# Attention and expert layer on one core: the order of ScalarE's high parts, GpSimd's low parts and scattered rows, and SyncE's copy of k

## The chip, the core and the metric

The kernel runs on one core of one Trainium2 chip. The metric is the device time of one execution in microseconds (us); of several executions the median is given. All times below are of that kind or come from one profiled execution.

## The reference, cut to what matters

The input x is 4 sequences of 512 tokens with 256 features. Attention has 32 query heads and 8 key/value heads of 64 features; both q and k are rotated by position. It is followed by a mixture of 8 experts with two chosen per token.

```
proj = layernorm(x) @ W_qkv
q, k, v = split(proj);  q = rope(q);  k = rope(k)
attn = einsum('bqhmd,bkhd->bhmqk', q, k) / 8
attn = where(q_pos >= k_pos and q_pos < k_pos + 64, -inf, attn)
w = softmax(concat([attn, sink]))[..., :-1]
x = x + einsum('bhmqk,bkhd->bqhmd', w, v).reshape(B, L, 2048) @ W_out
# experts: softmax gates, top 2 of 8, capacity 640 rows per expert
h = relu(rows_of_expert @ w1 + b1);  y = h @ w2 + b2
x = x + sum over the two experts of weight * y
```

Every large product is made of float32 operands split in a high part (rounded to the matmul's fp32r type) and a low part (the rest): three matmuls, high by high, low by high and high by low, stand for one.

## The kernel before

**Groups.** Attention is cut into 32 groups g (4 sequences by 8 key/value heads). A group has one key head, one value head and four query heads. Its projection comes in three chunks of 128 rows by 512 tokens: KV (k in rows 0 to 63, v in rows 64 to 127), Q01 and Q23 (two query heads each). Scores are made in 16 units of 128x512, two by two on TensorE (L1591), each followed by one VectorE instruction that masks and takes the maximum (L1185) and by one exponential on ScalarE (L895). VectorE then transposes pairs of units (L1196), and TensorE multiplies by v (L1617) and by W_out (L1649).

**The order written by hand.** Function `all_periods` (L364) walks g and a unit number n from 0 to 15. At each it calls, for each engine, the step of group g at n, then that of group g + 1 at n - 16, of g - 1 at n + 16 and of g - 2 at n + 32, then the routing of a finished sequence and other early work. So an entry "-15: KV" of a table stands in unit 1 of the group before. Each engine runs its own instructions in this order, and waits on semaphores in between; an entry sets an order on one engine and no time. I call the 16 units of group g "the period of g".

**The path of a chunk.** TensorE projects KV and Q01 of g + 1 in units 0 and 2 (`project_pair`, L1508) and Q23 in unit 10 (`project`, L1495, which waits for v's copy `s_v_next`). ScalarE copies each chunk out of PSUM into chunk_sb (`chunk_out`, L862, instruction L871). SyncE moves 16-row halves of it to swap_sb (`swap_halves`, L505, DMAs L511: two for KV, four for Q01 and Q23). GpSimd rotates: two products and one sum, L709, L710 and L714. ScalarE makes the high part (`qk_high`, L882, instruction L886), GpSimd the low part (`qk_low`, L717, instruction L720). k is needed in both halves of the partitions, so SyncE copies rows 0 to 63 of k's parts, 256 KB, to rows 64 to 127 (`k_twice`, L514, DMA L517). The first score of a group (L1591, n == 0) waits for Q01's low part, for that copy and for the maximum of the unit before. TensorE's product with v of the group before starts in unit 4 and waits, on its way, for the KV chunk's copy (L1611), since both use one PSUM bank.

**v.** ScalarE copies the turned v (`v_copy`, L879) in unit 9; SyncE writes it to memory and reads it back spread over partitions (L538, L546).

**SyncE's queue** per period, in order: reciprocals out and spread (L554, L562) of the group before, swaps of KV and Q01, in the first sequence weight loads and the writing of the weight parts, v out and in, swaps of Q23, then for the groups 8 to 31 the reading of the weight's high and low parts (`load_w_again`, L525, DMAs L530, two of 384 KB, issued three groups ahead), then `k_twice`:

```
                swap_halves(g + 1, Q23)
                if NKV <= g + 3 < GROUPS:
                    load_w_again(g + 3, (g + 3) % 2)
                k_twice(g + 1, (g + 1) % 2)
```

24 of the 31 copies of k stand behind such a pair of reads.

**ScalarE's queue** in a period, as far as the change goes: exponential 1, KV chunk out (g + 1), exponential 2, exponential 3, high part of Q23 (g), Q01 chunk out, ..., exponential 7, high part of k, exponentials 8 and 9, v's copy, exponential 10, high part of Q01, exponential 11, Q23 chunk out.

**GpSimd's queue**: denominator (L745), rotation and low part of Q23 (g), rotations of KV and Q01 (g + 1), low parts of k (unit 6) and of Q01 (unit 10), residual of g - 2 (L752, two instructions, unit 11), a weight's low part in the first sequence, sink argument (L735). `SCATTER_AT`, `ROOT_AT` and `GATE_EXP_AT` place the routing of a finished sequence, which runs beside the next one's eight groups: r counts its units, so r = 67 is unit 3 of the fifth group. `ROOT_AT` is a run of seven small GpSimd instructions (L765 to L772), `GATE_EXP_AT` eight small ScalarE instructions in two lots (L1072, L1074), `SCATTER_AT` eight indirect DMAs that GpSimd issues (L800), each with a wait for the spread reciprocals of an earlier group. `LATE_ROOT_AT` places two more such runs on GpSimd.

After the last group the routing of the last sequence and the eight experts run; the change moves no instruction there.

Of the kernel before, what the change touches and what calls it, by code (L numbers as in the profile page):

```python
# [39 lines left out]
UNITS = QM * TPB  # L40
# [15 lines left out]
KV, Q01, Q23 = 0, 1, 2  # L56
# [4 lines left out]
def moe_layer(nc, x, w_qkv, w_out, sink, gate_w, w1, b1, w2, b2, rope, out):  # L61
    ctx = ExitStack()
    with ctx:
# [276 lines left out]

        PROJ_PAIR_AT = {-16: 0, -14: 1}
        PROJ_AT = {-6: Q23}
        CHUNK_OUT_AT = {-15: KV, -13: Q01, -5: Q23}
        TURN_V_AT, V_NEXT_AT = -8, -7
        ROT_AT = {2: Q23, -12: KV, -11: Q01}
        QK_HI_AT, QK_LO_AT = {3: Q23, -9: KV, -6: Q01}, {3: Q23, -10: KV, -6: Q01}
        W_HI_AT, SPLIT_AT, SECOND_SPLIT_AT = -7, -3, -10
        PV_AT, at = {}, 0
        for n, blocks in [(20, 5), (22, 5), (24, 6)]:
# [3 lines left out]
        SINK_AT, DENOM_AT, RECIP_AT = 15, 16, 17  # L353
        HEADS_AT = 25
        Y_AT = {28: 0, 30: 1}
        Y_FIRST_OUT_AT, Y_OUT_AT, RESIDUAL_AT = 30, 31, 43
        ODD_ORDER = (1, 0)
        LAST_RESIDUAL_AT = {29: 0, 31: 1}

# [27 lines left out]
        LOGITS_AT, MEAN_PART_AT, STD_AT, TURN_LOGITS_AT, CENTRE_AT = 52, 53, 53, 54, 55  # L387
        TOP_AT, INDEX_AT = 56, 57
        ONEHOT_AT, COUNT_AT, RSTD_AT, PLACE_AT = 69, 70, 70, 71
        INV_STD_AT, ROOT_AT = 58, 67  # L390
        NORM2_AT, GATE_EXP_AT = {87: 0, 88: 1, 90: 2, 91: 3}, {71: (0, 1), 73: (2, 3)}
        SELECT_AT = 72
        PICK_AT, INDICES_AT, WEIGHTS_AT = 85, 86, 86
        SCATTER_AT = {89: (0, 1), 99: (2,), 105: (3, 4), 115: (5,), 121: (6, 7)}
        ROUTE_STEPS = 122

        def mean_part_of(eng):
# [19 lines left out]
        LATE_VAR_AT = {UNITS + 5: 0, 6 * UNITS + 5: 1}  # L417
        LATE_STD_AT = {UNITS + 5: 0, 6 * UNITS + 7: 1}
        LATE_INV_AT = {UNITS + 10: 0, 6 * UNITS + 10: 1}
        LATE_ROOT_AT = {2 * UNITS + 3: 0, 7 * UNITS + 3: 1}  # L420
        LATE_PERIODS = [3, 4, 5, 6, 8, 9, 13, 14, 15, 16, 17, 22]
        LATE_NORM_AT = {p * UNITS + 2: i for i, p in enumerate(LATE_PERIODS)}
        LATE_TURN_AT = {p * UNITS + 4: i for i, p in enumerate(LATE_PERIODS)}
# [50 lines left out]
        def rotated(q):  # L474

            return q - CHUNKS + 1
# [9 lines left out]
        def _(sp):  # L486
# [6 lines left out]
            def load_w(g, j):  # L493

                if later(g - 1):
                    sp.wait_ge(s_w_lo, g - 1)
                k = g % NKV
                sp.dma_start(w_raw[j][:, :, 0:QM * HD],
                             w_rows[:, :, bass.ds(k * (QM * HD), QM * HD)]).then_inc(s_w_in[j], 16)
                sp.dma_start(w_raw[j][:, :, QM * HD:QM * HD + HD],  # L500
                             w_rows[:, :, bass.ds(k * HD + QW, HD)]).then_inc(s_w_in[j], 16)
                sp.dma_start(w_raw[j][:, :, QM * HD + HD:GW],
                             w_rows[:, :, bass.ds(k * HD + (QW + KW), HD)]).then_inc(s_w_in[j], 16)

            def swap_halves(g, c):  # L505

                q = g * CHUNKS + c
                sp.wait_ge(s_chunk_out, q + 1)
                for base in (0,) if c == KV else (0, HD):
                    for to, of in ((0, HD // 2), (HD // 2, 0)):  # L510
                        sp.dma_start(swap_sb[c][base + to:base + to + RH, :],  # L511
                                     chunk_sb[c][base + of:base + of + RH, :]).then_inc(s_swapped[c], 16)

            def k_twice(g, j):  # L514

                sp.wait_ge(s_qk_lo, rotated(g * CHUNKS + KV))
                sp.dma_start(qk[j][HD:P, :, PAIRS, :].bitcast(F32), qk[j][0:HD, :, PAIRS, :].bitcast(F32)).then_inc(s_k_twice, 16)  # L517

            def keep_w(g, j):

                sp.wait_ge(s_w_lo, g + 1)
                for part, w in enumerate((w_hi, w_lo)):
                    sp.dma_start(w_parts[g, part], w[j][:, :, :].rearrange("p c n -> p (c n)").bitcast(F32)).then_inc(s_w_kept[j], 16)
# [9 lines left out]
            def v_out(g):  # L533

                sp.wait_ge(s_v_next, g + 1)
                if g > 0:
                    sp.wait_ge(s_v_in[(g - 1) % 2], ((g - 1) // 2 + 1) * (16 * QUADS))
                sp.dma_start(v_rows, v_next[:, :, :].rearrange("p t d -> p (t d)")).then_inc(s_v_out, 16)  # L538

            def v_in(g, j):  # L540

                sp.wait_ge(s_v_out, g * 16 + 16)
                if later(g - 1):
                    sp.wait_ge(s_pv, g - 1 + 1)
                for a in range(QUADS):
                    sp.dma_start(v_quads[j][a * BLK:(a + 1) * BLK, :, :],  # L546
                                 v_rows.rearrange("(c j) n -> j c n", j=BLK)).then_inc(s_v_in[j], 16)

            def recip_out(g):

                sp.wait_ge(s_recip, g + 1)
                if g > 0:
                    sp.wait_ge(s_recip_in, g * 32)
                sp.dma_start(recip_rows, recip_t[:, :]).then_inc(s_recip_out, 16)  # L554

            def recip_spread(g):

                sp.wait_ge(s_recip_out, g * 16 + 16)
                if later(2 * g):
                    sp.wait_ge(s_heads, 2 * g + 1)  # L560
                for p in range(PAIRS):
                    sp.dma_start(recip_wide[p * HD:(p + 1) * HD, :, :].rearrange("p a (c i) -> p a c i", i=BLK),  # L562
                                 recip_rows.rearrange("(x a c) i -> x a c i", x=1, a=QUADS)[:, :, p * 8:p * 8 + 8, :]
                                 .broadcast_to([HD, QUADS, 8, BLK])).then_inc(s_recip_in, 16)
# [14 lines left out]
            def out_init(b):  # L579

                sp.wait_ge(s_residual, (b + 1) * 2 * NKV)
                sp.dma_start(out_rows[:, b * TPB:(b + 1) * TPB, :],
                             x_sb[:, b * TPB:(b + 1) * TPB, :]).then_inc(s_out_init, 16)

            for g in range(GROUPS - 1):
                if g > 0:
                    recip_out(g - 1)
                    recip_spread(g - 1)
                swap_halves(g + 1, KV)
                swap_halves(g + 1, Q01)  # L590
                if g + 1 < NKV:
                    keep_w(g + 1, (g + 1) % 2)
                if g + 3 < NKV:
                    load_w(g + 3, (g + 3) % 2)
                v_out(g + 1)
                v_in(g + 1, (g + 1) % 2)
                swap_halves(g + 1, Q23)
                if NKV <= g + 3 < GROUPS:
                    load_w_again(g + 3, (g + 3) % 2)
                k_twice(g + 1, (g + 1) % 2)  # L600
                if g % NKV == 1 and g > NKV:
                    out_init(g // NKV - 1)

# [41 lines left out]
        def _(pool):  # L645
# [128 lines left out]
            def pool_route(r, b, last):  # L774
# [10 lines left out]
                if r == IDS_AT:  # L785
                    if b > 0:
                        pool.wait_ge(s_scattered, b * (16 * TPB * TOPK))
                    nc.gpsimd.iota(xn2[:, :, D:D + 1].bitcast(U32), pattern=[[P, TPB], [0, 1]], base=b * L,
                                   channel_multiplier=1).then_inc(s_ids, 1)
                for c in SCATTER_AT.get(r, ()):  # L790
                    if not last:
# [22 lines left out]
            def pool_ahead(m):  # L814
                if m in LATE_ROOT_AT:
                    i = LATE_ROOT_AT[m]
                    part = LATE_PARTS[i]
# [27 lines left out]
        def _(act):  # L845
# [42 lines left out]
            def act_step(n, g, j):  # L888
                if n in CHUNK_OUT_AT:
                    chunk_out(g, CHUNK_OUT_AT[n])  # L890
                if n == V_NEXT_AT:
# [954 lines left out]
```

## Time and profile before

| what | value |
|---|---|
| median of 3 runs | 1327.89 us (1326.34 to 1331.36) |
| profiled execution: its own time | 1333.01 us |
| profiled execution: span from first to last instruction | 1331.2 us |
| mean granted TensorE clock | 0.905 of full |
| TensorE (PE) busy | 1077.3 us, 81% of the span |
| VectorE (DVE) busy | 934.6 us, 70% |
| GpSimd (POOL) busy | 711.1 us, 53% |
| ScalarE (ACT) busy | 708.6 us, 53% |
| chain that ended last, by engine | PE 45%, issue 13%, DMA 13%, POOL 8%, ACT 8%, DVE 7%, SyncE's queue 5% |

PE, DVE, ACT and POOL are the four computing engines, SP is SyncE, and a q behind a name means the engine's sequencer, which issues DMAs. A timeline row gives the start in us from the span's start, the length in us, engine, line, operation, what is written from what is read, the shapes and the count; in square brackets stand the idle time of the engine before it and what ended that time. The profiled execution is 0.4% longer than the median of the runs.

### The profile page before, as it was taken

Reading aid. Unit: us, or ns where it says so; the run is one execution under the profiler, and the core shown is the slowest. Engines: PE = TensorE matmul, PEld = TensorE weight load, DVE = VectorE, ACT = ScalarE, POOL = GpSimd, SP = SyncE. Lnnn points to the kernel's source line nnn. Section 1 sums busy time; section 2 is a strip of 40 time slices with the busy share of each in tenths; the row PEclk is TensorE's granted clock in tenths of the full one; section 3 lists DMA queues with packets and bytes.
Section 4 is the critical chain, followed back from the end, with each engine's and each line's share of the span. In section 5 each row is a group of like instructions: output and inputs, shape, how many; then the busy total and the mean of one; then the engine's idle time right before and its main releaser. Section 6 shows DMA issues by size and latency. Waiting matters only on the chain.

```text
span 1331.2 us, 33592 instructions
## 1 busy us (share of the span) xinstructions
PE 1077.3 (81%) x13509; PEld 844.5 (63%) x13509; DVE 934.6 (70%) x1962; ACT 708.6 (53%) x1769; POOL 711.1 (53%) x646
## 2 busy tenths in 40 slices
PE   7778777777687688787877777787777989999997
PEld 4457555555465566665665555565555669999996
DVE  7788777666577777776777676767677567777664
ACT  5566655555365455654665555546555445554442
POOL 4677664555455556654565666545557523224332
PEclk9899888888788888988888888888889999999998
DMA  5544543433322233323222333323333244433441
GB/s 146 148 119 138 147 125 106 109 100 92 88 74 82 72 92 95 103 81 92 77 81 73 100 99 97 106 83 88 83 99 84 69 165 110 111 100 100 106 105 21
DMA packets 107195, 131.98 MB, mean 99 GB/s; under 512 B 22848, under 2 KB 85376, under 8 KB 106912
## 3 DMA queue, kind: packets, MB, share of 16 engines
q1 hardware_dynamic: 89264, 110.08, 28.9%
q0 software_dynamic: 7296, 8.55, 3.9%
q10 hardware_dynamic: 10480, 11.20, 2.8%
q8 instruction: 107, 1.75, 0.5%
q14 instruction: 48, 0.39, 0.1%
HBM read 84.28 MB, written 28.12 MB: 84 GB/s over the span
## 4 chain that ended last, share of the span: by engine, by line
PE 45%; issue 13%; DMA 13%; POOL 8%; ACT 8%; DVE 7%; SPq 5%; ACTq 0%; POOLq 0%; DVEq 0%
PE bank L1782 9%; PE bank L1591 8%; DMA swap_sb<-chunk_sb 6%; PE bank L1649 6%; PE bank L1793 5%; PE bank L1617 5%; PE bank L1524 4%; ACT probs_ring L895 4%; DMA qk<-qk 4%; PE bank L1504 3%; SPq L511 3%; PE bank L1796 3%; POOL chunk_sb L714 2%; POOL chunk_sb L709 2%; POOL swap_sb L710 2%
## 5 line engine op out<-in xcount | busy, mean ns | idle before, releaser
L1185 DVE CUSTOM_DVE_ANT_0 probs_ring<-bank,mask,sink_neg 128x512 f32<-128x512 f32 x512 | 361.8, 740 | 244.4 <-PE bank L1591 233.5
L895 ACT ACTIVATE probs_ring<-probs_ring,neg_max 128x512 f32<-128x512 f32 x512 | 364.8, 714 | 296.6 <-DVE neg_max L1185 293.8
L1591 PE MATMUL bank<-qk 64*128 64x512 f32 x1488 | 266.7, 466 | 178.6 <-issue 112.8
L1196 DVE STREAM_TRANSPOSE probs_t<-probs_ring 128x1024 f32<-128x1024 f32 x256 | 317.4, 1240 | 6.2 <-ACT probs_ring L895 5.9
L1591 PEld LDWEIGHTS bank<-qk 64*128 64x128 f32 x1488 | 151.6, 212 | 253.6 <-issue 215.4
L720 POOL TENSOR_TENSOR qk<-chunk_sb,qk 128x512 fp32r<-128x512 f32 (+1 forms) x93 | 119.1, 1284 | 287.8 <-ACT qk L886 287.5
L1617 PE MATMUL bank<-probs_t,v_quads 32*64 32x256 f32 x8192 | 259.9, 388 | 3.9 <-issue 0.3
L1617 PEld LDWEIGHTS bank<-probs_t,v_quads 32*64 32x64 f32 x8192 | 189.9, 134 | 57.8 <-issue 37.4
L835 POOL DMA_INDIRECT out<-expert_sb,slots x40 | 77.5, 1938 | 154.1 <-DVE expert_sb L1448 147.4
L709 POOL TENSOR_TENSOR chunk_sb<-chunk_sb,rope_sb 128x512 f32<-128x512 f32 (+1 forms) x94 | 119.7, 1273 | 73.7 <-DMA swap_sb<-chunk_sb 73.4
L714 POOL TENSOR_TENSOR chunk_sb<-chunk_sb,swap_sb 128x512 f32<-128x512 f32 (+1 forms) x93 | 118.6, 1276 | 7.3
L710 POOL TENSOR_TENSOR swap_sb<-swap_sb,rope_sb 128x512 f32<-128x512 f32 (+1 forms) x94 | 119.7, 1273 | 0.0
L1104 ACT ACTIVATE hidden<-bank,b_sb 128x320 f32<-128x320 f32 x128 | 60.5, 525 | 110.5 <-PE bank L1782 107.7
L1649 PE MATMUL bank<-wo_sb,heads_sb 64*128 64x256 f32 x992 | 118.1, 378 | 0.0
L1793 PE MATMUL bank<-w_part,hidden_hi 128*128 128x512 f32 x320 | 114.9, 400 | 0.0
L1524 PE MATMUL bank<-xcur,w_hi 64*128 64x512 f32 x496 | 106.9, 507 | 0.0
L1649 PEld LDWEIGHTS bank<-wo_sb,heads_sb 64*128 64x128 f32 x992 | 96.4, 189 | 14.5
L886 ACT ACTIVATE qk<-chunk_sb 128x512 fp32r<-128x512 f32 (+1 forms) x93 | 57.9, 622 | 79.5 <-POOL chunk_sb L714 79.3
L895 ACT ACTIVATION_READ_ACCUMULATOR probs_ring<-probs_ring,neg_max 128x1 f32 x512 | 96.1, 188 | 0.0
L871 ACT ACTIVATE chunk_sb<-bank 128x512 f32<-128x512 f32 x94 | 55.0, 585 | 76.8 <-PE bank L1524 75.4
L1796 PE MATMUL bank<-w_part,hidden_lo 128*128 128x256 f32 x320 | 90.1, 282 | 0.0
L752 POOL TENSOR_TENSOR x_sb<-x_sb,y_sb 128x512 f32<-128x512 f32 x62 | 79.4, 1280 | 4.4
(193 smaller groups left out, 1545.4 us busy)
## 6 DMA issues: line engine op xcount, KB each, us to landing
v_quads<-v_rows SPq DMA_DIRECT2D x128, 128.0 KB
recip_wide<-recip_rows SPq DMA_DIRECT2D x64, 256.0 KB, 4.4
w_raw<-in_L_ffn_w SPq DMA_DIRECT2D x14, 1024.0 KB, 8.7
swap_sb<-chunk_sb SPq DMA_DIRECT2D x314, 32.0 KB, 2.5
w_hi<-w_parts SPq DMA_DIRECT2D x24, 384.0 KB, 3.5
w_lo<-w_parts SPq DMA_DIRECT2D x24, 384.0 KB, 4.8
qk<-qk SPq DMA_DIRECT2D x31, 256.0 KB, 4.9
slots<-slot_rows SPq DMA_DIRECT2D x9, 662.5 KB, 4.0
```

The costliest lines, as they stand in the source:

```text
L709: nc.gpsimd.tensor_tensor(straight, straight, rope_sb[rows, 0, :], ALU.mult).then_inc(s_pool, 1)
L710: nc.gpsimd.tensor_tensor(swapped, swapped, rope_sb[rows, 1, :], ALU.mult).then_inc(s_pool, 1)
L714: nc.gpsimd.tensor_tensor(qk_first[:, c - Q01, :] if g == 0 else straight, straight, swapped, ALU.add).then_inc(s_rot, 1)
L895: nc.scalar.activation(probs[(g * UNITS + n) % RING][:, :], probs[(g * UNITS + n) % RING][:, :], ACT.Exp, bias=neg_max[j][:, n:n + 1], sca ...
L1185: nc.vector.tensor_tensor_reduce(probs[(g * UNITS + n) % RING][:, :], SCORE[SCORE_OF[n // 2][n % 2]][:, :], mask[:, L - P - t * P:2 * L - ...
L1196: nc.vector.transpose(probs_t[:, pair_slot(g, h // 2), :, :] .rearrange("p b (h q) -> p h b q", h=2)[:, :, :, t * BLK:(t + 1) * BLK], prob ...
L1524: ins = nc.tensor.matmul(chunk_bank(c)[:, :], w[rows, kc, chunk_cols(c)], xcur[g // NKV % 2][rows, part, kc, :], start=(second == 0 and kc ...
L1591: ins = nc.tensor.matmul(out_bank, qk[j][half, q_part, h // 2, t * P:(t + 1) * P], qk[j][half, k_part, PAIRS, :], start=(m == 0), stop=(m ...
L1617: ins = nc.tensor.matmul(PV[a][p * HD:(p + 1) * HD, 0:2 * P], v_quads[j][rows, d, c * HD:(c + 1) * HD], probs_t[rows, pair_slot(g, p), blk ...
L1649: ins = nc.tensor.matmul(PV[a][:, 0:D], heads_sb[rows, a, h * P:(h + 1) * P], wo_sb[rows, (g % NKV) * 2 + h, :], start=(half == 0 and h == ...
L1793: nc.tensor.matmul(FFN2[s][:, :], hidden_hi[:, c, s * P:(s + 1) * P], w2_parts[e % 2][:, c, :, :].rearrange("p t d -> p (t d)"), start=(c ...
L1796: ins = nc.tensor.matmul(FFN2[s][:, 0:D], hidden_lo[:, c, s * P:(s + 1) * P], w2_hi[e % 2][:, c, :], start=False, stop=(c == HC - 1))
```

## The change

It moves entries of the hand-written order. ScalarE: KV chunk out from unit 1 to unit 2, the high part of Q23 from unit 3 to 2 (there it comes ahead of the KV chunk), the high part of k from 7 to 8 (behind exponential 8). GpSimd: the low part of Q01 from unit 10 to 7, the residual from 11 to 8, the routing's root from unit 3 to 6 of its period, the scatters of r = 99 and 115 to 91 and 107 (from unit 3 of a period to unit 11 of the one before), the two late roots by four units. ScalarE's gate exponentials go from units 7 and 9 to 12 and 14. SyncE issues k's copy ahead of the two reads of weight parts.

```
-        CHUNK_OUT_AT = {-15: KV, -13: Q01, -5: Q23}
+        CHUNK_OUT_AT = {-14: KV, -13: Q01, -5: Q23}
-        QK_HI_AT, QK_LO_AT = {3: Q23, -9: KV, -6: Q01}, {3: Q23, -10: KV, -6: Q01}
+        QK_HI_AT, QK_LO_AT = {2: Q23, -8: KV, -6: Q01}, {3: Q23, -10: KV, -9: Q01}
-        Y_FIRST_OUT_AT, Y_OUT_AT, RESIDUAL_AT = 30, 31, 43
+        Y_FIRST_OUT_AT, Y_OUT_AT, RESIDUAL_AT = 30, 31, 40
-        INV_STD_AT, ROOT_AT = 58, 67
-        NORM2_AT, GATE_EXP_AT = {87: 0, 88: 1, 90: 2, 91: 3}, {71: (0, 1), 73: (2, 3)}
+        INV_STD_AT, ROOT_AT = 58, 70
+        NORM2_AT, GATE_EXP_AT = {87: 0, 88: 1, 90: 2, 91: 3}, {76: (0, 1), 78: (2, 3)}
-        SCATTER_AT = {89: (0, 1), 99: (2,), 105: (3, 4), 115: (5,), 121: (6, 7)}
+        SCATTER_AT = {89: (0, 1), 91: (2,), 105: (3, 4), 107: (5,), 121: (6, 7)}
-        LATE_ROOT_AT = {2 * UNITS + 3: 0, 7 * UNITS + 3: 1}
+        LATE_ROOT_AT = {2 * UNITS + 7: 0, 7 * UNITS + 7: 1}
...
                 swap_halves(g + 1, Q23)
+                k_twice(g + 1, (g + 1) % 2)
                 if NKV <= g + 3 < GROUPS:
                     load_w_again(g + 3, (g + 3) % 2)
-                k_twice(g + 1, (g + 1) % 2)
```

## Rows read from the trace of the kernel before

**Rows 1.** Waits: who waited for what, us in total, times, longest us.

```profile
PE bank L1591 <- issue: 112.8, 21, 8.5
...
POOL chunk_sb L709 <- DMA swap_sb<-chunk_sb: 73.4, 33, 7.6
PE bank L1591 <- DMA qk<-qk: 56.0, 10, 9.0
```

**Rows 2.** Timeline of PE, 541 to 577 us, the period of group 16.

```profile
542.20 1.65 PE L1591 MATMUL bank<-qk 64*128 64x512 f32 x6 [5.28 <-issue]
...
548.83 2.42 PE L1617 MATMUL bank<-probs_t,v_quads 32*64 32x256 f32 x80
...
561.04 0.73 PE L1504 MATMUL bank<-xcur,w_hi 128*128 128x512 f32 x2 [0.91 <-ACT v_next L879]
...
573.38 1.65 PE L1591 MATMUL bank<-qk 64*128 64x512 f32 x6 [5.65 <-issue]
```

**Rows 3.** Timeline of SyncE's queue in the same stretch.

```profile
549.60 4.67 SPq L511 DMA_DIRECT2D swap_sb<-chunk_sb  x6
...
564.49 2.42 SPq L511 DMA_DIRECT2D swap_sb<-chunk_sb  x4
567.01 0.53 SPq L530 DMA_DIRECT2D w_hi<-w_parts  x1
...
568.06 0.67 SPq L517 DMA_DIRECT2D qk<-qk  x1
```

**Rows 4.** k's copy in the stretches 370:970, 190:340 (5 copies), 568.1:568.2, 990:1030 (2), 40:170 (5).

```profile
L517 SPq DMA_DIRECT2D qk<-qk x19: 660/661/665, 372.4 to 963.4; - x19
...
DMA to landing us min/median/max: 4.4/4.9/5.6
...
DMA to landing us min/median/max: 5.8/6.8/7.0
...
DMA to landing us min/median/max: 5.2/5.2/5.2
...
DMA to landing us min/median/max: 3.1/3.1/3.1
...
DMA to landing us min/median/max: 3.1/4.1/5.4
```

**Rows 5.** Timeline of ACT, 541 to 577 us.

```profile
548.09 0.60 ACT L871 ACTIVATE chunk_sb<-bank 128x512 f32<-128x512 f32 x1 [1.92 <-PE bank L1524]
...
550.49 0.61 ACT L886 ACTIVATE qk<-chunk_sb 128x512 fp32r<-128x512 f32 x1
...
558.67 0.63 ACT L886 ACTIVATE qk<-chunk_sb 64x512 fp32r<-64x512 f32 x1 [2.74 <-POOL chunk_sb L714]
...
560.62 0.36 ACT L879 ACTIVATE v_next<-bank 128x256 f32<-128x256 f32 x1
```

**Rows 6.** Timeline of DVE, unit 2 of group 16.

```profile
546.75 0.71 DVE L1185 CUSTOM_DVE_ANT_0 probs_ring<-bank,mask,sink_neg 128x512 f32<-128x512 f32 x1
```

**Rows 7.** Timeline of POOL: k's rotation, Q01's last step, a scatter, group 30's Q23.

```profile
554.78 1.28 POOL L709 TENSOR_TENSOR chunk_sb<-chunk_sb,rope_sb 64x512 f32<-64x512 f32 x1 [2.32 <-DMA swap_sb<-chunk_sb]
...
561.19 1.30 POOL L714 TENSOR_TENSOR chunk_sb<-chunk_sb,swap_sb 128x512 f32<-128x512 f32 x1
...
522.94 1.01 POOL L800 DMA_INDIRECT slot_rows<-xn,scatter_idx  x1 [1.62 <-DMA swap_sb<-chunk_sb]
...
1001.00 1.29 POOL L714 TENSOR_TENSOR chunk_sb<-chunk_sb,swap_sb 128x512 f32<-128x512 f32 x1
```

**Rows 8.** Timeline of ACT around the first gate exponentials, group 12.

```profile
426.21 0.38 ACT L1072 ACTIVATE gates<-logits,neg_top,rstd 128x8 f32<-128x8 f32 x1
...
427.71 0.70 ACT L895 ACTIVATE probs_ring<-probs_ring,neg_max 128x512 f32<-128x512 f32 x1
```

**Rows 9.** Busy time by stretch: PE, PEld, DVE, ACT, POOL, then granted clock, DMA.

```profile
573.40:579.40 6.00, 6.00 (x28) 5.14 (x30) 3.46 (x8) 1.52 (x4) 0.00 (x0) 0.50 0.02 3
997.90:1003.90 6.00, 5.80 (x59) 4.88 (x67) 5.05 (x13) 4.03 (x13) 4.04 (x4) 1.00 0.03 7
```

## The prediction

> **What bounds the kernel now.** I read the waits first: of everything TensorE waits for in the attention part, the first score of a group stands out, with 112.8 us in 21 waits put down to "issue" and 56.0 us in 10 put down to k's copy [rows 1]. Together that is 168.8 us in 31 waits, one for each of the 31 copies. Are they one thing? The timeline of one period says so. TensorE starts group 17 at 573.38 us after 5.65 us of nothing, that is, its last work ended at 567.73 [rows 2]. SyncE issued the copy at 568.06 [rows 3], and it landed 5.2 us later, at 573.26 [rows 4]: 0.12 us before the score. So "issue" hides the same wait, and each group starts when k's second half has landed.
>
> What holds the copy? In SyncE's queue it comes last: four swaps of Q23 from 564.49, the two reads of weight parts from 567.01, then the copy [rows 3]. k itself is long ready: its rotation began at 554.78 and GpSimd's rotation of Q01 was done at 562.49 [rows 7], with k's low part next in its queue. The reads cost the copy twice: their issue, 568.06 - 567.01 = 1.05 us, and the transfer, for the copy's 256 KB go behind 768 KB. The 19 copies behind such reads from group 10 on land in 4.4/4.9/5.6 us, the two last ones, which have none ahead, in 3.1 [rows 4].
>
> **The change, part by part.** The sum is made against the profiled execution, 1333.0 us.
>
> *k's copy ahead of the weight parts.* 24 copies gain 1.05 us of issue: 25.2 us. Their landing shortens too. For the 19 the ends are 3.1 us (as the two without reads) and 4.9 (as now, if packets issued 0.7 us later still share the way). I take 3.4, close to the lower end, since what is issued ahead of the copy is then just what stands ahead of the two at 3.1: 19 x 1.5 = 28.5 us. The five copies from 190 to 340 us land in 6.8 us in the median [rows 4]; there ScalarE also writes zero rows. The five copies before them, with no read ahead but partly beside such writes, take 3.1/4.1/5.4. The ends are 3.1 and 6.8, and I take 4.7: 5 x 2.1 = 10.5 us. Sum 64.2 us. The reads now land about when the next group starts, two periods ahead of their use, and the swaps on which the next chain rests go out 7.4 us after such a start (549.60 - 542.20, [rows 2, 3]): nobody waits. What is late next: TensorE's own work ends at 567.73; the copy, issued at 567.01 and landed at 570.4, still comes 2.7 us later. So the copy stays the bound and the gain is kept whole.
>
> The Trainium skill ("DMA: Bandwidth & Descriptors", Queues, rings and completion order) says that each engine takes descriptors in ring order, but that data descriptors carry no barrier. By the ring order alone the 19 would land in 3.1 us and give 5.7 us more; by free mixing they would stay at 4.9. The trace agrees with the order as far as 3.1 against 4.9 goes; no run here yet shows reads issued behind a copy.
>
> *ScalarE: KV out behind exponential 2 and Q23's high part.* VectorE ends unit 2 at 547.46 [rows 6]. An exponential of 0.70 [rows 8] and the high part's 0.61 [rows 5] follow, so KV's copy starts near 548.8 instead of 548.09 [rows 5]: 0.7 us late. Two wait for it. TensorE's product with v started at 548.83, 0.14 us behind the copy's end [rows 2, 5], and moves by 0.7. SyncE's first swap went out at 549.60 [rows 3], the copy now ends near 549.4, so it does not move here; where TensorE's clock is low and unit 2 ends later it would, by up to 0.5.
>
> *k's high part behind exponential 8.* ScalarE waited 2.74 us for the rotation [rows 5]; exponential 8 now fits into that, and v's copy comes 0.70 us earlier, at 559.9. TensorE waited 0.91 us for it [rows 2], so that takes up the 0.7 us that it lost. And Q23's chunk is copied behind Q01's high part, which waits for GpSimd until 562.49 [rows 7], and nothing here moved that. So in this period both edits cancel. In others the v path or TensorE decides. Bounds per period: -0.3 (0.7 less for v against 0.4 more on the swap's path) and +0.7, for 30 periods -9 and +21; I take +0.15 each, the value nearest to this period's: +5 us.
>
> *GpSimd.* In an ordinary period the new numbers change no order: nothing stands between units 7 and 11 but the low part and the residual. So "low parts behind both rotations" is true already: cost 0, covered by nothing, as there is nothing to cover. Only the routing's pieces really move. Two scatters per routed sequence, six in all, stood ahead of k's rotation, 1.01 us each [rows 7], partly while GpSimd waited for the swap anyway: up to 6 us, I take 2. The new place is behind the residual, where GpSimd has slack until the sink argument. The gate exponentials, first lot 427.71 - 426.21 = 1.5 us [rows 8], stood ahead of exponential 8 and v's copy in three periods: up to 4.5 us, I take 3. The roots stood just ahead of a rotation, where GpSimd waits for a swap anyway, 73.4 us in 33 waits or 2.2 us each [rows 1]; moved behind the rotations, their seven small instructions bring between 0 and, had that wait been used up, their own length; I take 0. The residual ahead of scatters that wait: 0.
>
> Sum: 64.2 - 5 + 2 + 3 = 64 us, so 1269 us for that execution. The median of the runs was 0.4% (5.1 us) lower, so I give 1327.9 - 64 = **1264 us**.
>
> **The rivals.** *The landing does not shorten* (8%): reads issued 0.7 us behind the copy share its way. Then only the issue is won, 25 us: 1303 us. For it: all use the same 16 engines. Against: the bytes ahead of the copy are gone, and 3.1 us is what it takes without them.
>
> *The clock rises too* (9%). A group now starts at the lower level, 1.2 GHz, after some 5.7 us of idle: 0.50 in the first 6 us; at the start of group 30, whose copy had landed in 3.1 us, it stayed at 1.00, 2.4 GHz [rows 4, 9]. With 2.7 us of idle some starts may stay high. The first six matmuls took 1.65 us at the low level [rows 2], half of that could go: with the units behind them about 0.8 us in 24 periods, 19 us, 1245 us. Against: the low stretch may only move into the middle of the period. The Trainium skill ("TensorE: Matmul & The Clock Gate", HAM oscillation) tells of this kind of loss from waits between bursts; by it the shorter wait would help, which rows 9 neither show nor exclude for 2.7 us.
>
> *The copy is not what releases the score* (4%): something else always comes 0.1 us before. Then the time is 1328 + 5, no change. Against: 31 waits for 31 copies, and the 0.12 us between landing and score.
>
> *Slower* (2%): Q23's high part now stands ahead of KV out, and its rotation ends late when groups start early. In group 30 it ended at 1002.29 [rows 7], 4.4 us after TensorE's start at 997.9 [rows 9]. ScalarE now wants it 6.0 us after the start (547.46 + 0.70 against 542.20, [rows 2, 6, 8]), somewhat sooner at the high clock. Beyond that each us is paid by KV out, its swap and the whole next chain. The sign turns where that wait passes 64 / 30 = 2.1 us, at a rotation end of 8.1 us: at 9.2 us the price is 3.2 x 30 = 96 us against 64, 1360 us. Against: nothing in the change delays Q23's swaps.
>
> **The numbers.** My forecast holds 77%, with its own range from the bounds: the 19 landings at 3.1 (6 us) and ScalarE's edits at -0.2 per period (10 us), to all landings 0.6 us longer (14 us) and ScalarE's edits at +0.5 (11 us): 1248 to 1289. All terms at their ends at once would give 1231 (landings 14, ScalarE 14, GpSimd and gates 5 us) and 1324 (39, 16 and 5), which is wider than 8 in 10 asks for. The range 1244 to 1289 takes the clock case in and leaves out the unshortened landing, no change, and slower: 14%, plus tails. About 0.5% is what a measurement of this kernel can tell from no change. Faster by more: 77 + 8 + 9 = 94%; same 4%, slower 2%.
>
> **What would show it.** In the changed profile: k's copies issued right behind the swaps of Q23, all landing near 3.4 us; TensorE's waits ahead of the first score down from 169 to about 105 us; periods of ordinary groups of 28 to 29 us instead of 31.2 (573.38 - 542.20, [rows 2]); KV out 0.7 us later in its period, with the product with v as well, and v's copy 0.7 earlier; no scatter ahead of a rotation. I am wrong if the copies still take 4.9 us, if the score is released by anything else, or if ScalarE waits for Q23's rotation in unit 2.

## The result, and the profile after

The changed kernel takes **1217.46 us** (median of 3 runs, 1217.24 to 1218.3) against 1327.89: ratio 0.9173 [0.9139, 0.9208]. The forecast was 1264, with a range from 1244 to 1289. The direction was right, the size was not: the gain is 110 us, not 64, and the time lies 27 us below the range.

The head of the changed kernel's page (cut):

```profile
span 1215.5 us, 33592 instructions
...
PE 1045.4 (86%) x13509; PEld 832.0 (68%) x13509; DVE 928.1 (76%) x1962; ACT 710.0 (58%) x1769; POOL 713.5 (59%) x646
```

TensorE's busy time fell by 32 us (1077.3 before) though it does the same work: it ran at a higher clock, 0.941 of full speed granted against 0.905.

Waits of the changed kernel, to hold against [rows 1]:

```profile
PE bank L1591 <- DMA qk<-qk: 78.4, 23, 4.8
PE bank L1591 <- issue: 28.0, 8, 4.6
PE bank L1617 <- ACT chunk_sb L871: 20.9, 30, 1.6
PE bank L1504 <- ACT v_next L879: 12.9, 9, 6.5
```

The first scores wait 106.4 us in 31 waits, where 168.8 stood: the forecast said "about 105". Of the fourth row it gave no sum. Here are that row and one more of the kernel before; the second matters below:

```profile
PE bank L1504 <- ACT v_next L879: 34.1, 21, 5.8
...
PE bank L1542 <- ACT x2T L1064: 8.2, 3, 3.0
```

k's copy in the changed kernel, in 190:330 (5 copies) and 330:870 (19), to hold against [rows 4]:

```profile
L517 SPq DMA_DIRECT2D qk<-qk x5: 654/655/1176, 193.2 to 310.6; - x5
DMA to landing us min/median/max: 3.2/3.4/4.9
...
L517 SPq DMA_DIRECT2D qk<-qk x19: 654/655/659, 341.9 to 855.9; - x19
DMA to landing us min/median/max: 3.1/3.2/3.3
```

The same period of group 16, SyncE's queue and then TensorE, to hold against [rows 2, 3]:

```profile
512.62 2.42 SPq L511 DMA_DIRECT2D swap_sb<-chunk_sb  x4
515.08 0.65 SPq L517 DMA_DIRECT2D qk<-qk  x1
515.83 0.54 SPq L530 DMA_DIRECT2D w_hi<-w_parts  x1
```

```profile
490.53 0.97 PE L1591 MATMUL bank<-qk 64*128 64x512 f32 x6 [3.09 <-DMA qk<-qk]
...
493.57 1.54 PE L1591 MATMUL bank<-qk 64*128 64x512 f32 x6
...
497.85 2.42 PE L1617 MATMUL bank<-probs_t,v_quads 32*64 32x256 f32 x80 [0.62 <-ACT chunk_sb L871]
...
518.39 1.21 PE L1591 MATMUL bank<-qk 64*128 64x512 f32 x6 [3.06 <-DMA qk<-qk]
```

The period is 518.39 - 490.53 = 27.86 us long, 31.18 before and 28 to 29 in the forecast; the copy stands right behind the swaps. From group start to the copy's issue it takes 24.55 us (25.86 before), from there to the next start 3.31 (5.32 before). The first six matmuls take 0.97 us, not 1.65: this group starts at 2.4 GHz. The half speed comes later: the scores at 493.57 took 1.54 us, and the first six microseconds stand at a granted clock of 0.72, not at 0.50 as in [rows 9]:

```profile
490.40:496.40 6.00, 5.87 (x38) 5.52 (x40) 4.25 (x10) 2.90 (x9) 4.00 (x4) 0.72 0.43 160
```

Not every group is like this one. I call a start cold when its first six matmuls took over 1.3 us (1.65 is the value at 1.2 GHz, 0.97 that at 2.4). Of the 31 starts 28 were cold before and 17 still are. Idle of 3.03 us ahead of group 15 was followed by 1.65 us, idle of 3.09 us ahead of group 16 by 0.97.

The chain from start to start can be summed over the 30 full periods of a trace, in three pieces: from a group's first VectorE instruction to the issue of k's copy, from there to the copy's landing (the last arrival recorded for its semaphore), and from there to the next group's first VectorE instruction. In us, with the cold starts beside:

| kernel | start to issue | issue to landing | landing to start | sum | cold starts of 31 |
|---|---|---|---|---|---|
| before | 774.8 | 149.7 | 50.2 | 974.7 | 28 |
| changed | 723.8 | 100.2 | 42.3 | 866.2 | 17 |
| e1, copy alone | 749.2 | 104.4 | 38.8 | 892.4 | 12 |
| e2, k's high part alone | 756.1 | 149.3 | 50.3 | 955.8 | 28 |
| e3, all but the copy | 760.2 | 154.0 | 50.5 | 964.6 | 28 |
| e4, all but k's high part | 748.9 | 103.3 | 40.7 | 892.8 | 15 |
| e10, one read ahead | 746.2 | 134.4 | 50.8 | 931.3 | 29 |
| e11, filling matmuls | 711.4 | 101.1 | 33.1 | 845.6 | 2 |

Between the kernel before and the changed one, start to issue fell by 51 us, issue to landing by 49.5, landing to start by 8. The sum of 108.5, with some 7 us ahead of and behind these periods, is the difference of the spans, 1331.2 - 1215.5 = 115.7. In both traces all 31 first scores start 0.1 us after the landing of k's copy.

### The profile page after: what moved, and what is told of

Its sections match the earlier page's. It is cut to its first block and busy times, and to the rows that moved or that the text cites. A ratio compares the mean times of both kernels' runs of the same rounds, so it can differ in the third digit from the quotient of the medians.

```text
span 1215.5 us, 33592 instructions
## 1 busy us (share of the span) xinstructions
PE 1045.4 (86%) x13509; PEld 832.0 (68%) x13509; DVE 928.1 (76%) x1962; ACT 710.0 (58%) x1769; POOL 713.5 (59%) x646
## 5 line engine op out<-in xcount | busy, mean ns | idle before, releaser
L1591 PE MATMUL bank<-qk 64*128 64x512 f32 x1488 | 259.4, 454 | 112.0 <-DMA qk<-qk 78.4
L1591 PEld LDWEIGHTS bank<-qk 64*128 64x128 f32 x1488 | 148.0, 204 | 183.4 <-issue 147.7
L1617 PE MATMUL bank<-probs_t,v_quads 32*64 32x256 f32 x8192 | 249.1, 380 | 23.9 <-ACT chunk_sb L871 20.9
L1617 PEld LDWEIGHTS bank<-probs_t,v_quads 32*64 32x64 f32 x8192 | 186.6, 132 | 71.0 <-DVE probs_t L1196 32.9
L720 POOL TENSOR_TENSOR qk<-chunk_sb,qk 128x512 fp32r<-128x512 f32 (+1 forms) x93 | 118.7, 1281 | 108.5 <-ACT qk L886 108.3
L714 POOL TENSOR_TENSOR chunk_sb<-chunk_sb,swap_sb 128x512 f32<-128x512 f32 (+1 forms) x93 | 119.3, 1283 | 7.3
L710 POOL TENSOR_TENSOR swap_sb<-swap_sb,rope_sb 128x512 f32<-128x512 f32 (+1 forms) x94 | 120.5, 1282 | 0.0
L1524 PE MATMUL bank<-xcur,w_hi 64*128 64x512 f32 x496 | 103.4, 486 | 0.0
L1782 PE MATMUL bank<-slots_hi,w_hi 128*128 128x320 f32 x256 | 79.4, 310 | 0.0
L1782 PE MATMUL bank<-slots_lo,w_hi 128*128 128x320 f32 x256 | 79.0, 308 | 0.0
```

What stands on the lines that cost most here:

```text
L710: nc.gpsimd.tensor_tensor(swapped, swapped, rope_sb[rows, 1, :], ALU.mult).then_inc(s_pool, 1)
L714: nc.gpsimd.tensor_tensor(qk_first[:, c - Q01, :] if g == 0 else straight, straight, swapped, ALU.add).then_inc(s_rot, 1)
L1591: ins = nc.tensor.matmul(out_bank, qk[j][half, q_part, h // 2, t * P:(t + 1) * P], qk[j][half, k_part, PAIRS, :], start=(m == 0), stop=(m ...
L1617: ins = nc.tensor.matmul(PV[a][p * HD:(p + 1) * HD, 0:2 * P], v_quads[j][rows, d, c * HD:(c + 1) * HD], probs_t[rows, pair_slot(g, p), blk ...
L1782: ins = nc.tensor.matmul(banks[4 + 2 * (c % 2) + half][:, 0:HALF], w[:, kc, c * P:(c + 1) * P], a[:, at:at + HALF], start=(kc == 0 and m = ...
```

## The experiments

They ran in four batches, each beside runs of the kernel before on the same chip (medians 1331.77, 1340.82, 1333.75 and 1336.55 us), so ratios are compared, not times. Two add matmuls whose result is not used, e11 and e15; all others only reorder.

### Which edit carries the gain

**e1**, the kernel before with the copy's edit alone:

```diff
                 swap_halves(g + 1, Q23)
+                k_twice(g + 1, (g + 1) % 2)
                 if NKV <= g + 3 < GROUPS:
                     load_w_again(g + 3, (g + 3) % 2)
-                k_twice(g + 1, (g + 1) % 2)
```

> The kernel before with k's copy ahead of the two reads of weight parts, and nothing else. Theory A (each edit has its own part): the order of the copy gives the landings (about 48 us over 24 copies), the issue (25 us) and a little of TensorE's clock at the group starts (up to 8 us), so 73 to 81 us of the 110: 1247 to 1255 us. Rival B (the earlier start alone shifts everything, ScalarE's and GpSimd's edits do nothing): 1215 to 1225 us. Rival C (the forecast on record for this part, landings of 3.4 and 4.7 us): 64 us, 1264 us.

**e3**, the changed kernel with SyncE's order put back:

> The changed kernel with the copy of k put back behind the reads. Theory A: the gain of all but the copy, 110 - 77 = about 33 us, shows alone: 1288 to 1302 us. Rival B: nothing of it without the copy's edit: 1322 to 1332 us. Forecast on record for these parts: 1328 us.

**e2**, the kernel before with k's high part behind exponential 8, and **e4**, the changed kernel with it back in unit 7:

```diff
-        QK_HI_AT, QK_LO_AT = {3: Q23, -9: KV, -6: Q01}, {3: Q23, -10: KV, -6: Q01}
+        QK_HI_AT, QK_LO_AT = {3: Q23, -8: KV, -6: Q01}, {3: Q23, -10: KV, -6: Q01}
```

> The kernel before with only the high part of k moved from unit 7 to unit 8 on ScalarE. Theory A: what stood behind its wait in unit 7 (the turned x of three periods, norms, gate exponentials) is released, about 4 us in each of three periods with x turned, 1 to 2 us in the three with gate exponentials, and some of an exponential's 0.7 us elsewhere: 15 to 25 us faster, 1303 to 1313 us. Rival (forecast on record: the edits on ScalarE cancel): 1323 to 1333 us.

> The changed kernel with k's high part back in unit 7. Theory A: it loses 15 to 25 us, 1232 to 1243 us, with TensorE waiting about 3 us for the second turned x in the periods of groups 10, 18 and 26 again. Rival B: same time as the changed kernel, 1215 to 1221 us.

| kernel | ratio to before | interval |
|---|---|---|
| changed | 0.9173 | 0.9139 to 0.9208 |
| e1, copy alone | 0.9352 | 0.9285 to 0.9419 |
| e3, all but the copy | 0.9848 | 0.9777 to 0.9919 |
| e2, k's high part alone | 0.984 | 0.9777 to 0.9904 |
| e4, all but k's high part | 0.9338 | 0.9273 to 0.9404 |

The copy's edit is worth 1 - 0.9352 = 0.0648, 86 us of 1331.77, by itself, and 0.9848 - 0.9173 = 0.0675, 90 us, on top of the others. k's high part is worth 0.016 and 0.0165, 21 and 22 us, where the forecast had let it cancel with KV out and booked a loss of 5 for both. 86 + 21 = 107 of 110 us: the two edits carry nearly the whole gain, and they add. The intervals of these four runs reach 0.006 to 0.007 to either side, some 9 us, so the 21 us can be told from no effect, but their size is rough. e2 and e4 came out as expected. On the scale of the first runs, e1 (1242 us) was 5 us faster than its theory, and e3 (1308) missed its 1288 to 1302. With the copy's edit alone the waits are these:

```profile
PE bank L1504 <- ACT v_next L879: 52.3, 23, 7.7
PE bank L1591 <- issue: 47.5, 22, 4.8
PE bank L1591 <- DMA qk<-qk: 32.1, 8, 5.4
```

First scores 79.6 us in 30 waits. But Q23's projection (L1504) now waits 52.3 us for v's copy, 34.1 before: what k's copy gave up, v's copy partly took. In e2 that wait is 17.0 us in 14, but the first scores there wait 186.8 us in 32, 18 more than before: in e2 an earlier projection of Q23 mostly met a copy of k that was not earlier.

**e5 and e16**, the changed kernel with KV out and Q23's high part put back; **e6 and e17**, with all of GpSimd's entries and the gates put back. Each was run twice in different batches, and **e14** is the changed kernel once more:

```diff
-        CHUNK_OUT_AT = {-14: KV, -13: Q01, -5: Q23}
-        QK_HI_AT, QK_LO_AT = {2: Q23, -8: KV, -6: Q01}, {3: Q23, -10: KV, -9: Q01}
+        CHUNK_OUT_AT = {-15: KV, -13: Q01, -5: Q23}
+        QK_HI_AT, QK_LO_AT = {3: Q23, -8: KV, -6: Q01}, {3: Q23, -10: KV, -9: Q01}
```

> The changed kernel with KV's chunk out back in unit 1 and Q23's high part back in unit 3. Forecast on record: these edits cost about 0.15 us per period (bounds -0.3 to +0.7 together with k's high part), so undoing them gives up to 15 us, 1203 to 1215 us. Rival (nothing waits for them): 1215 to 1220 us, with TensorE's product with v again 0.14 us behind KV's copy and starting 0.6 us sooner in its period. Second rival (they help, as exponential 2 no longer waits): 1222 us or more.

> The changed kernel with KV out in unit 1 and Q23's high part in unit 3, against the changed kernel on the same chip. TensorE's product with v waits 21 us in all for KV's copy in the changed kernel, but most of that is taken up by later waits: 0 to 8 us faster (ratio 0.911 to 0.917). If this edit had been a gain: ratio above 0.920.

> The changed kernel with all of GpSimd's entries and the gate exponentials as before (low part of Q01, residual, roots, gate exponentials, scatters); ScalarE's KV out and high parts and the order of k's copy stay changed. Forecast on record: 5 us (scatters 2, gates 3), so 1222 us. Theory A: k's high part in unit 8 has already released what the gate exponentials held up (they now come after the wait is used up), 1217 to 1221 us. Rival (GpSimd's order matters): 1230 us or more.

> The changed kernel with GpSimd's entries and the gate exponentials as before, against the changed kernel on the same chip: 3 to 13 us slower (ratio 0.919 to 0.927). If they do nothing: 0.915 to 0.919.

> The changed kernel itself, beside the three others on one chip, as their reference: a ratio of 0.917 to the kernel before within its interval.

Measured: e5 0.9127 [0.9078, 0.9176], e16 0.9149 [0.9103, 0.9195]; e6 0.9197 [0.9144, 0.9249], e17 0.9209 [0.9169, 0.9249]; e14 0.9178 [0.9142, 0.9214]. Against 0.9173 and 0.9178, ScalarE's edit looks like a loss of 0.003 to 0.005 (4 to 6 us) and GpSimd's like a gain of 0.002 to 0.003 (3 to 4 us). Every interval overlaps the changed kernel's, so neither is told apart from nothing. The traces say a little more. The sum over the 30 periods is 866.2 and 866.4 us in the two profiles of the changed kernel, 861.4 and 866.6 in those of e5 and e16, and 878.9 in both of e6 and e17: GpSimd's edits with the gates lean to a gain, of some 4 us by the ratios and 13 by these four profiles. Which of its five edits would bring it, no run separates.

### Why k's high part is worth 21 us

The forecast looked at an ordinary period. Periods in which a sequence is routed have one more piece behind k's high part in ScalarE's queue: the second half of the turned x (L1064, unit 7). TensorE's turn of v (L1542) stands behind it. Group 10 of the kernel before, ScalarE and then TensorE:

```profile
356.81 0.63 ACT L886 ACTIVATE qk<-chunk_sb 64x512 fp32r<-64x512 f32 x1 [2.49 <-POOL chunk_sb L714]
357.35 0.57 ACT L1064 ACTIVATE x2T<-bank 128x512 f32<-128x512 f32 x1
```

```profile
358.07 0.66 PE L1542 MATMUL bank<-identity,chunk_sb 64*128 64x64 f32 x4 [2.98 <-ACT x2T L1064]
358.65 5.42 PE L1617 MATMUL bank<-probs_t,v_quads 32*64 32x256 f32 x96
```

ScalarE waited 2.49 us for GpSimd's rotation of k with the turned x standing behind it in the queue, TensorE waited 2.98 us for that piece, and then its 96 matmuls took 5.42 us, at 1.2 GHz. In the changed kernel the piece goes first, and the same 96 take 2.85. The window of the kernel before (granted clock 0.50), then ScalarE and TensorE of the changed kernel:

```profile
357.50:364.10 6.60, 6.03 (x102) 3.64 (x102) 0.32 (x1) 2.10 (x6) 4.33 (x5) 0.50 0.06 22
```

```profile
330.76 0.57 ACT L1064 ACTIVATE x2T<-bank 128x512 f32<-128x512 f32 x1
...
333.24 0.62 ACT L886 ACTIVATE qk<-chunk_sb 64x512 fp32r<-64x512 f32 x1
```

```profile
331.48 0.43 PE L1542 MATMUL bank<-identity,chunk_sb 64*128 64x64 f32 x4
331.85 2.85 PE L1617 MATMUL bank<-probs_t,v_quads 32*64 32x256 f32 x96
```

**e8** tests that reading from the other side. k's high part stays, and the turned x is put ahead of it in the kernel before:

```diff
-        TURN_X_AT, X2T_AT = {36: 0, 38: 1}, {37: 0, 39: 1}
+        TURN_X_AT, X2T_AT = {36: 0, 38: 1}, {37: 0, 38: 1}
```

> The kernel before with only the second half of the turned x (ScalarE's copy L1064) moved from unit 7 to unit 6 of its period, ahead of k's high part. If that copy behind k's wait is what stops TensorE in the periods of groups 10, 18 and 26 (2.98 us idle in the first, and a product with v at the low clock behind it), they lose about 4 us each as in the run with k's high part in unit 8 (4.6, 3.6, 3.6): 12 us, about 1315 to 1320 us, and those periods are 31 to 33.5 us long. If k's high part has to move itself, nothing: 1327 to 1333 us.

Measured 0.9902 [0.9869, 0.9936], 13 us (9 to 18). Group 10 of e8:

```profile
357.03 0.60 ACT L1064 ACTIVATE x2T<-bank 128x512 f32<-128x512 f32 x1 [1.75 <-PE bank L1708]
...
358.78 0.63 ACT L886 ACTIVATE qk<-chunk_sb 64x512 fp32r<-64x512 f32 x1 [0.45 <-POOL chunk_sb L714]
```

The three periods themselves show it, from one group's first score to the next one's, in us:

| group | before | e2 | e8 |
|---|---|---|---|
| 10 | 37.15 | 32.55 | 33.22 |
| 18 | 35.93 | 32.38 | 32.17 |
| 26 | 34.75 | 31.12 | 30.75 |
| sum gained | | 11.8 | 11.7 |

So the piece queued behind k's high part is worth 12 us in either run. The 30 periods of e2 gain 18.9 us together. Of the other 7.1, 4.5 fall in group 13 (36.79 before, 32.28 in e2) and 2.6 in the other 26 periods together, 0.1 each. Some 7 us of the difference between those two profiles lie outside the periods. In the changed order it is otherwise: e4 loses 26.6 us against the changed kernel, 13.0 in groups 10, 18 and 26 and the rest spread over others, with 21.6 us of waits for v's copy where 12.9 stood. That v's copy carries that rest is likely, but no run separates it.

Group 13 stays in part unexplained. A small VectorE instruction there took 3.49 us before and 0.19 in the changed kernel:

```profile
457.65 3.49 DVE L406 TENSOR_TENSOR xn<-gates,top_sum 128x32 f32<-128x32 f32 x1
```

```profile
416.01 0.19 DVE L406 TENSOR_TENSOR xn<-gates,top_sum 128x32 f32<-128x32 f32 x1
```

Before, GpSimd's rotation of k ran beside it. In the traces of all runs but e15 this instruction took 0.88 us or more (1.03 in e2, 1.12 in e8) wherever the second or third step of a rotation (L710, L714) ran beside it, and 0.19 everywhere else. That is only observed; no run separates it, and the changed kernel taken once more (e14) has 1.12 in group 13. Its 3.49 - 1.03 = 2.5 us are over half of what e2 gained in that period.

### How much the reads cost, and the clock

**e10**, the changed kernel with the first read (384 KB) ahead of the copy and the second behind it:

> The changed kernel with the read of the high weight parts (384 KB) again ahead of k's copy, that of the low parts behind it: half the dose. If issue and bytes ahead set the landing, the copy goes out 0.57 us later and lands in about 4.2 us instead of 3.2, so each of 24 periods is 1.5 us longer, 36 us, plus a few us of clock at the starts: 1250 to 1260 us. If only the place in the queue's issue counts and not the bytes: 14 us, 1231 us. If the step from two reads to one brings nothing (a threshold): 1300 us.

Measured 0.9614 [0.9574, 0.9654], 0.0441 more than the changed kernel, 59 us for one read in 24 periods. SyncE's queue and TensorE in e10:

```profile
609.94 0.53 SPq L531 DMA_DIRECT2D w_hi<-w_parts  x1
610.51 0.66 SPq L517 DMA_DIRECT2D qk<-qk  x1
611.26 0.54 SPq L531 DMA_DIRECT2D w_lo<-w_parts  x1
```

```profile
614.97 1.65 PE L1594 MATMUL bank<-qk 64*128 64x512 f32 x6 [4.80 <-DMA qk<-qk]
```

(The edit adds three lines to the kernel, so L1591 is L1594 here.) In this period the start comes 4.46 us after the issue, not 3.3, and after 4.80 us of idle it runs at 1.2 GHz: 1.65 us. Over all 30 periods, by the table of pieces, e10 is longer than the changed kernel by 22 us from start to issue (24 x 0.57 = 14 of them are the read's own issue), by 34 from issue to landing, and by 8 from landing to start: 65 us in the profiled executions, 59 by the ratios. e10's copies land in 4.6 us in the median, those of the changed kernel in 3.2. The expectation, 36 us and a little of clock, was missed: it had 1.0 us more per landing and little for the clock. The landings took 1.4 us more, and 29 of 31 starts are cold, where 17 were.

The second read adds 33 us in the same sums (e3 against e10): 14, 20 and nothing. So the first read costs two thirds of what both do: more than half of issue and landing, and the whole of the clock at the starts.

**e11** fills the wait ahead of each first score with matmuls whose result is not used:

```diff
+                            pe.wait_ge(s_chunk_out, (g + 1) * CHUNKS)
+                            keep_warm(2, PROJ, rope_sb[:, 0, :])
```

> The changed kernel with two more matmuls (identity by a constant table, into the projection's free bank, result unused) ahead of each group's first score, in TensorE's wait for k's copy. Theory on the clock: the idle stretch of some 3 us is what lets the granted clock fall to 1.2 GHz at the starts; filled, the starts run at 2.4 GHz and the first six matmuls take 1.0 instead of 1.65 us in the 18 or so periods where they were slow: 10 to 20 us faster, 1198 to 1207 us. Rival (the dummies hold up the score, or the low stretch moves elsewhere): 1215 to 1225 us.

Measured 0.9008 [0.8959, 0.9058], 0.0165 or 22 us faster than the changed kernel. The wait for the copy is still there, issue to landing as long as before (101.1 us against 100.2) and each first score 0.1 us behind a landing. What the filling gave back is the half speed behind the waits: 2 cold starts, not 17. The granted clock is 0.979:

```profile
core 0: 1198.9 us, clock 0.979
```

### A better place for the copy

In the changed kernel the copy still stands behind Q23's four swaps, 2.42 us of issue. **e12** puts it ahead of them. **e13** does so too and puts KV out and Q23's high part back to units 1 and 3. **e15** is e13 with one filling matmul ahead of each first score, where e11 has two.

```diff
+                k_twice(g + 1, (g + 1) % 2)
                 swap_halves(g + 1, Q23)
-                k_twice(g + 1, (g + 1) % 2)
```

> The changed kernel with k's copy one place further ahead, before the four swaps of Q23. k's low part is ready about 20 us into a period and the swaps begin at 21, so the copy would go out 2.4 us sooner and land at about 24.4 us, near the end of TensorE's own work at 24.5 to 25. If the copy is still the bound, 1.5 to 2.5 us per period in 30 periods: 45 to 75 us, 1142 to 1172 us. Rival (Q23's rotation, now 0.7 us later and with earlier starts, holds ScalarE in unit 2, where KV out waits behind it): half of it is given back, 1180 to 1200 us.

> The same with KV's chunk out back in unit 1 and Q23's high part back in unit 3, so nothing stands behind Q23's rotation in unit 2. If that rotation holds ScalarE in the run before this one, this one is 10 to 30 us faster than it; if it does not, they are equal within 5 us.

> k's copy ahead of Q23's swaps, KV out in unit 1 and Q23's high part in unit 3, with one more matmul ahead of each group's first score. In the run without it the gaps ahead of the first score are down to about 1 us and the clock is at 2.4 GHz nearly always, so the clock theory expects nothing more from it: ratio within 0.005 of that run's 0.857. Rival (any filling still helps): 0.845 or less. If the dummy now holds up the score, 0.865 or more.

Measured: e12 0.8994 [0.895, 0.9038], 1200.86 us; e13 **0.8574 [0.8541, 0.8608], 1141.59 us**; e15 0.8535 [0.8503, 0.8568], 1139.7 us. e13 beats both kernels clearly; e15's interval overlaps e13's, so filling adds nothing there that can be told apart. For e12 the expectation was 1142 to 1172 us; its rival came true. For e13 it was 10 to 30 us less than e12, and the difference is larger.

e12 and e13 ran side by side and differ by the one ScalarE edit (KV out and Q23's high part), 0.042 or 56 us. e12's waits, then one of them, ScalarE and TensorE:

```profile
PE bank L1617 <- ACT chunk_sb L871: 66.5, 30, 5.0
```

```profile
493.80 0.63 ACT L886 ACTIVATE qk<-chunk_sb 128x512 fp32r<-128x512 f32 x1 [0.95 <-POOL chunk_sb L714]
494.33 0.58 ACT L871 ACTIVATE chunk_sb<-bank 128x512 f32<-128x512 f32 x1
```

```profile
495.06 3.41 PE L1617 MATMUL bank<-probs_t,v_quads 32*64 32x256 f32 x72 [2.04 <-ACT chunk_sb L871]
```

Q23's swaps go out later behind the copy, and the next group starts earlier. Q23's high part, in unit 2, waits for the rotation; KV out stands behind it, and TensorE's product with v behind that. This is the forecast's "slower" rival, mechanism and place, called up by the earlier copy. With the edit put back (e13) that wait is 1.1 us in 4, and the start shown waits 0.73 us:

```profile
463.98 0.66 SPq L517 DMA_DIRECT2D qk<-qk  x1
464.68 2.65 SPq L511 DMA_DIRECT2D swap_sb<-chunk_sb  x4
```

```profile
467.93 0.97 PE L1591 MATMUL bank<-qk 64*128 64x512 f32 x6 [0.73 <-issue]
```

```profile
PE bank L1504 <- ACT v_next L879: 34.2, 27, 4.3
...
PE bank L1591 <- issue: 27.0, 22, 3.4
...
PE bank L1591 <- DVE neg_max L1185: 13.7, 29, 2.1
...
PE bank L1591 <- DMA qk<-qk: 6.7, 5, 2.0
```

v's copy is TensorE's largest named wait there. But "issue" hides k's copy again: by the recorded arrivals of the copy's semaphore, 26 of the 31 first scores start within 0.25 us of its landing. The copy still releases most starts, with TensorE's own work ending only about 1 us earlier. And it lands later, in 3.8 us in the median (3.7 in e12), where it took 3.2 with the reads right behind it instead of the swaps; no run shows why.

## Why the prediction was wrong

**What bounds the kernel: right.** Each start waited for the copy, "issue" hiding most of it: all 31 first scores come 0.1 us after a landing, before and in the changed kernel. Undoing the SyncE edit alone takes back 90 of 110 us, so the rival that the copy is not the releaser is out.

**The copy's issue: right.** 25.2 us forecast; the copy now goes out right behind the swaps. In e1 the sum from start to issue fell by 25.6. That it fits so closely is in part luck, for this piece also holds what the higher clock gave back and what the longer waits for v's copy took (52.3 us, 34.1 before).

**The copy's landing: right mechanism, wrong size.** The rival that it would not shorten is out: 3.2 and 3.4 us in the median, with two reads issued right behind. The forecast took 3.4 and 4.7. By the medians the changed kernel's landings gain 19 x 1.7 + 5 x 3.4 = 49.3 us, against 39.0: 10 us short. The rule of the Trainium skill ("DMA: Bandwidth & Descriptors", Queues, rings and completion order), by which the 19 would come to 3.1, agrees with 3.1/3.2/3.3. That transfers issued behind would cost the copy nothing holds for these reads and not throughout: with the four swaps right behind it, in e12 and e13, the copy took 3.7 and 3.8 us in the median.

**The clock: a rival where it belonged in the sum.** In e1 landing to start fell by 11 us over 30 periods: 12 cold starts, not 28, and the first six matmuls of all groups took 11 us less. The rival had put 19 us on this and 9% on its case, and the likeliest sum left it out, since the low stretch might only move. In the changed kernel both happened, group by group: 14 of 31 starts are not cold (3 before), and in group 16 the low stretch moved into the middle (1.54 us at 493.57). Issue, landing (45 in e1) and clock make 82 of the 88 us between the profiled executions of e1 and of the kernel before; 64 were booked. The Trainium skill ("TensorE: Matmul & The Clock Gate", HAM oscillation) tells of such losses from waits between bursts; e11, 22 us faster for filling them, agrees.

**k's high part: the step that failed.** "In this period both edits cancel. In others the v path or TensorE decides", and "+0.15 each" for both edits: +5 us. Group 16's waits were carried to all 30 periods with bounds of -0.3 and +0.7 each. Undoing k's high part costs 22 us and undoing KV out gives about 5, so both together gained some 17 us, 0.6 per period: outside the bounds. For ordinary periods the step was not far off in the order before: in e2, 26 of 30 periods gained 0.1 us each. What failed is that one period stood for all. What stands behind k's high part in ScalarE's queue was not listed for the routed periods, where 8.2 us in 3 waits of L1542 showed it; those three periods alone gained 12 us, in e2 as in e8. Group 13 gave 4.5 more in e2. And with k's copy early the same edit was worth more in the other periods too (13.6 us in e4), for which nothing in the sum stood.

**KV out and GpSimd: not refuted.** About +5 and -4 us, each within the intervals. In the changed kernel KV out makes TensorE wait 20.9 us in 30 waits, 0.7 each as forecast. In e5 and e16 that wait is gone, but those for v's copy are 26.7 and 25.3 us where the changed kernel has 12.9. So most of the 0.7 is taken up by a later wait, much as the forecast had it for group 16.

The errors add up. By undoing them, the copy's edit is worth 90 us, k's high part 22, KV out about -5, GpSimd about 4: 111 of the 110 measured. Booked were 64 for the copy, -5 for ScalarE and 5 for the rest. So the copy's landing and the clock were 26 short, ScalarE 22, and the rest 1 over: 47, against 46.5 measured between 1264 and 1217.46. The range left ScalarE's gain out entirely, and all terms at their fast ends at once (1231) would not have reached the result either.

One part of the profile difference stays open: a block of 80 matmuls in group 31 of the kernel before took 5.28 us at a granted clock of 1.00, where 2.41 is usual. It is not there in e1, e2 or the changed kernel's first profile, but it is in the changed kernel's second (e14, 4.50 us), so it does not belong to the change. No run explains it.

## What to carry to other kernels

In a hand-ordered queue the cost of a waiting instruction is what stands behind it in every kind of period, rare ones included: sum the waits of all who depend on it before one period is taken for all. A small transfer that releases the next burst of work goes ahead of large ones that nobody needs soon. It may then go ahead of the next thing in its queue too, as long as what it passes has slack. Each change of this kind shifts which order is best for the others: the same ScalarE edit was within noise (about 5 us) in one order of SyncE's queue and cost 56 us in the next. And before a wait is called gone, compare landing and start: a wait put down to "issue" was k's copy in the first kernel and again in the fastest one.

## What the runs showed of the hardware

k's copy of 256 KB landed in 3.1/3.2/3.3 us (least, median, most of 19) with 768 KB issued right behind it on the same queue, 0.1 us slower than with none beside it, 3.1 [rows 4]. With the four swaps of 32 KB right behind it, the median was 3.7 us (e12) and 3.8 (e13). With 768 KB ahead it was 4.9, with 384 KB ahead 4.6 (e10).

How long TensorE idled did not alone decide its clock afterwards. In the kernel before, 28 of 31 starts were cold, after 2.60 us of idle or more, and the three others came after 0.90, 1.39 and 2.44. In the changed kernel, after 2.9 to 3.3 us, some took 1.65 us for the first six matmuls (3.03 us of idle, group 15) and some 0.97 (3.09 us, group 16), and after the latter a later six took 1.54. Filled with matmuls whose result is not used, the idle of some 3 us ahead of 31 starts gave back 22 us, though the waits themselves stayed (e11).
